# A graph-network kernel: all loops written out, seven gathers for every pair of groups, and the eighth tile divided between ScalarE, VectorE and SyncE

## What is computed

```python
msg_in = jnp.concatenate([nodes[row], nodes[col], edge_features], axis=-1)
messages = relu(msg_in @ mW1 + mb1) @ mW2 + mb2
aggregated = jax.ops.segment_sum(messages, col, num_segments=12500)
upd = relu(jnp.concatenate([nodes, aggregated], -1) @ uW1 + ub1) @ uW2 + ub2
out = layernorm(nodes + upd)          # over the 64 features, no affine part
```

## Time and profile before

| | |
|---|---|
| median of 3 runs | 1922.34 us (1921.92 to 1922.72) |
| profiled execution, own time | 1922.22 us |
| its span, first to last instruction | 1920.4 us |
| granted TensorE clock, mean share of full speed | 0.804 |
| busy in the span | VectorE 1540.8 us, POOL 1431.4, TensorE 1429.3, ScalarE 1242.0 |
| DMA | 229.86 MB, 120 GB/s, 44% of 16 engines' time from 100 us on |

### The profile page before, as it was taken

How to read it: one execution, slowest core, us unless ns; L and a number is a source line. 1 busy time by engine, 2 the same in 40 slices (tenths; PEclk the granted TensorE clock), 3 DMA queues, 4 the chain that set the end, 5 groups by cost and what they waited for, 6 DMA issues and landing times.

```text
span 1920.4 us, 56413 instructions
## 1 busy us (share of the span) xinstructions
PE 1429.3 (74%) x8716; PEld 1334.2 (69%) x8716; DVE 1540.8 (80%) x10793; ACT 1242.0 (65%) x10165; POOL 1431.4 (75%) x1527
## 2 busy tenths in 40 slices
PE   6776677777678777767768777776867878777877
PEld 6776566777667677666667667766767767766776
DVE  5568888888888888888888888888888888888883
ACT  3246766767766766766666666766666666766663
POOL 7777777777777777777777777777777777777773
PEclk8898888778877878788887887878788776877686
DMA  9664444444444444444444444444444444444441
GB/s 239 163 154 113 123 114 114 123 115 114 123 113 114 124 115 112 120 118 113 115 123 113 112 122 117 114 119 120 112 115 123 113 114 122 115 114 119 118 109 35
DMA packets 169379, 229.86 MB, mean 120 GB/s; under 512 B 98508, under 2 KB 117687, under 8 KB 168701
## 3 DMA queue, kind: packets, MB, share of 16 engines
q1 hardware_dynamic: 112484, 124.14, 23.4%
q0 software_dynamic: 48416, 97.68, 20.6%
q10 hardware_dynamic: 8254, 5.59, 1.2%
HBM read 217.59 MB, written 9.60 MB: 118 GB/s over the span
## 4 chain that ended last, share of the span: by engine, by line
POOL 63%; issue 23%; PE 4%; DVE 3%; DMA 3%; DVEq 1%; ACT 1%; POOLq 1%; SPq 1%; ACTq 0%
POOL gath L717 63%; DVE col_x L469 2%; DMA gath<-table_src,idx 1%; PE ps_sum L856 1%; DVEq L460 1%; DMA table_src<-gath 1%; PE ps_pre L824 1%; PE ps_pre L825 1%; DVE hid L1180 1%; PE ps_pre L790 0%; PE ps_pre L832 0%; POOLq L302 0%; DMA xwin<-in_xT_dram 0%; ACT hid L1000 0%; DMA col_src<-in_srcT_dram 0%
## 5 line engine op out<-in xcount | busy, mean ns | idle before, releaser
L717 POOL DMA_INDIRECT gath<-table_src,idx x1388 | 1309.6, 944 | 423.0 <-issue 420.6
L469 ACT COPY col_x<-xdeg 64x1 f32 x9428 | 912.4, 187 | 237.6 <-issue 219.6
L832 PE MATMUL ps_pre<-rhs,lhs 128*128 128x128 f32 x3226 | 603.0, 363 | 448.3 <-DVE lhs L1158 445.6
L469 DVE COPY col_x<-xdeg 64x1 f32 x9408 | 718.2, 138 | 216.0 <-issue 215.5
L832 PEld LDWEIGHTS ps_pre<-rhs,lhs 128*128 128x128 f32 x3226 | 558.8, 269 | 477.1 <-DVE lhs L1158 473.9
L856 PE MATMUL ps_sum<-onehot,hid 128*128 128x96 f32 x3322 | 473.2, 304 | 13.0 <-ACT rhs L976 11.9
L856 PEld LDWEIGHTS ps_sum<-onehot,hid 128*128 128x128 f32 x3322 | 463.3, 221 | 23.5 <-issue 15.2
L1007 ACT ACTIVATE hid<-hid 128x1024 f32<-128x1024 f32 x202 | 212.5, 1052 | 180.4 <-DVE hid L1180 177.0
L1180 DVE TENSOR_TENSOR hid<-ps_pre,gath 128x1024 f32<-128x1024 f32 x202 | 246.4, 1220 | 87.2 <-DMA gath<-table_src,idx 75.4
L1158 DVE TENSOR_SCALAR_CACHE_REDUCE lhs<-lhs,place 96x1024 f32<-96x1024 int32 x208 | 264.6, 1272 | 32.7 <-PE ps_sum L765 19.8
L1150 DVE TENSOR_TENSOR onehot<-ps_iota,dst_rel 128x768 f32<-128x768 f32 (+1 forms) x209 | 196.9, 943 | 0.1
(11 more groups left out here) (109 smaller groups left out, 639.1 us busy)
## 6 DMA issues: line engine op xcount, KB each, us to landing
lhs<-in_dst_dram SPq DMA_DIRECT2D x207, 384.0 KB
lhs<-in_edgeT_dram SPq DMA_DIRECT2D x207, 128.0 KB
gath<-table_src,idx POOLq DMA_INDIRECT x1388
table_src<-gath SPq DMA_DIRECT2D x12, 512.0 KB, 7.0
xwin<-in_xT_dram SPq DMA_DIRECT2D x208, 24.0 KB
idx<-in_srcT_dram SPq DMA_DIRECT2D x192, 4.0 KB
out_dram<-yout ACTq DMA_DIRECT2D x48, 64.0 KB, 1.6
col_src<-in_srcT_dram SPq DMA_DIRECT2D x148, 0.5 KB
```

Of the source, the lines that this page charges most:

```text
L469: ins = copy(col_x[:, i, start + n + j:start + n + j + 1], col)
L717: pool.indirect_dma_start(gath[0:m, k, j * H:(j + 1) * H], None, table_src, src_by_tile(p, k, j, m)).then_inc(gathered[k], 16)
L832: mm = nc.tensor.matmul(to[0:m, j * H:(j + 1) * H], lhs[:, k, j * P:j * P + m], rhs[:, k, :], start=True, stop=not by_cols)
```

## The change

Four things are done together.

1. The `Fori` loops go. SyncE, POOL and ScalarE are written out like the others, and every number in them is a constant.
2. From pair 13 on every pair has seven gathers, slot 0 too. Of the eighth tile ScalarE copies columns 0 to 63, VectorE 64 to 119 (24, then 32), and the last 8 rows come as 8 DMAs of one `table_src` row each, issued by SyncE straight into `gath` (`load_rows`). Their places in `col_x` are zero.
3. ScalarE makes all its 64 copies for pair p+2 in one step. It loads its registers sixteen at a time, the first sixteen at the end of the step before. VectorE makes 32 copies for pair p+1 in the first batch and 24 for pair p+2 in the second; the wait for the second batch stands ahead of `turned`.
4. The starts of the windows are loaded four registers at a time at every fourth pair, in `add_sums` and in `load_window`, and VectorE computes the two addresses for `add_sums` (`place_sums`) ahead of its first batch. Indices are loaded into eight slots (`AHEAD`) instead of four, seven pairs ahead.

```diff
-COL_K = (1, 2, 3)
-COL_PLAN = (((2, 0, 32), (1, 48, 16)), ((2, 32, 32), (0, 0, 16)), ((0, 16, 32), (0, 48, 16)), ((1, 0, 32), (1, 32, 16)))
+EARLY = 16
+COL_FROM = 13
 COL_TILE = PT - 1
+COL_ACT = 64
+COL_LOAD = 16
+COL_DVE = 24
+COL_ROWS = 8
+AHEAD = 2 * SLOTS
...
-        def copy_batch(eng, copy, i, start, count, done):
+        def load_regs(eng, k, start, count):
             regs = [eng.alloc_register(f"col{next(col_regs)}") for n in range(count)]
-            eng.load(regs, col_src[0:1, i, start:start + count])
+            for n in range(0, count, 32):
+                eng.load(regs[n:n + 32], col_src[0:1, k, start + n:start + min(n + 32, count)])
+            return regs
...
+        def wait_cols(eng, p):
+            k = p % SLOTS
+            eng.wait_ge(col_src_in[k], col_loads(p))
+            if col_before(p) is not None:
+                eng.wait_ge(pe_steps, steps_for_pre(col_before(p)))
+            let(eng)
...
@@ SyncE
-            def load_idx(p, it, k):
-                if not (isinstance(p, int) and p < (PEELED + 1) * SLOTS):
-                    sp.wait_ge(hsum_made, p - SLOTS + 1)
+            def load_idx(p):
+                if p >= EARLY + AHEAD:
+                    sp.wait_ge(hsum_made, p - AHEAD + 1)
...
+                    if k == 0:
+                        regs = [sp.alloc_register(f"start{p + i}") for i in range(SLOTS)]
+                        sp.load(regs, start_i[0:1, p:p + SLOTS])
...
+                p = it * SLOTS + k
+                if has_cols(p + SLOTS):
+                    load_cols(p + SLOTS, col_tile(p + SLOTS), P)
...
+                if EARLY <= p + AHEAD - 1 < PAIRS:
+                    load_idx(p + AHEAD - 1)
+                if has_rows(p + PREP):
+                    load_rows(p + PREP, (k + PREP) % SLOTS)
...
+            def load_rows(p, k):
+                sp.wait_ge(col_src_in[k], col_loads(p))
+                sp.wait_ge(hsum_made, p - SLOTS + 1)
...
+                regs = [sp.alloc_register(f"row{next(col_regs)}") for n in range(COL_ROWS)]
+                sp.load(regs, col_src[0:1, k, P - COL_ROWS:P])
+                for n, reg in enumerate(regs):
+                    src = sp.snap(reg, donate=True, min_val=0, max_val=N - 1)
+                    q = P - COL_ROWS + n
+                    sp.dma_start(gath[q:q + 1, k, COL_TILE * H:PW], table_src[bass.ds(src, 1), :]).then_inc(rows_in[k], 16)
...
@@ ScalarE, in step
-                copy_cols(act, nc.scalar.copy, it, k, 0, 0, cols_act)
-                copy_cols(act, nc.scalar.copy, it, k, 1, 0, cols_act)
+                if has_cols(p + 2):
+                    if p + 2 == COL_FROM:
+                        first_regs(p + 2, to)
+                    held = act_regs.pop() + load_regs(act, to, COL_LOAD, COL_LOAD)
+                    copy_batch(act, nc.scalar.copy, to, 0, held)
+                    for start in range(2 * COL_LOAD, COL_ACT, COL_LOAD):
+                        held = load_regs(act, to, start, min(COL_LOAD, COL_ACT - start))
+                        done = copy_batch(act, nc.scalar.copy, to, start, held)
+                    done.then_inc(cols_act, 1)
+                if p + 2 >= COL_FROM and has_cols(p + 3):
+                    first_regs(p + 3, (k + 3) % SLOTS)
...
@@ VectorE, in step
-                copy_cols(dve, nc.vector.tensor_copy, it, k, 0, COL_HALF, cols_dve)
+                if p % SLOTS == SLOTS - 1:
+                    load_starts(p - SLOTS + 1)
+                at = place_sums(p - 3) if p >= 3 else None
+                if has_cols(p + 1):
+                    to, start = (k + 1) % SLOTS, COL_ACT + COL_DVE
+                    held = load_regs(dve, to, start, P - COL_ROWS - start)
+                    done = copy_batch(dve, nc.vector.tensor_copy, to, start, held)
...
+                if has_cols(p + 2):
+                    wait_cols(dve, p + 2)
...
-                    add_sums(*pair(it, k, 3))
+                    add_sums(*pair(it, k, 3), at)
...
-                copy_cols(dve, nc.vector.tensor_copy, it, k, 1, COL_HALF, cols_dve)
+                if has_cols(p + 2):
+                    to = (k + 2) % SLOTS
+                    held = load_regs(dve, to, COL_ACT, COL_DVE)
+                    copy_batch(dve, nc.vector.tensor_copy, to, COL_ACT, held).then_inc(cols_dve, 1)
```

More of the change, by code:

```diff
@@ L236, in gnn_kernel @@
         idx_rest_in = sem("idx_rest_in")
-        idx_in = [sem(f"idx_in{i}") for i in range(SLOTS)]
+        idx_in = [sem(f"idx_in{i}") for i in range(AHEAD)]
         raw_got = [sem(f"raw_got{i}") for i in range(RAW)]
@@ L357, in steps_for_window, with pairs @@
             return p - 2
-        def pairs(eng, step, node, tail, peeled=PEELED, looped=True):
-            for it in range(peeled if looped else LAG):
+        def pairs(eng, step, node, tail):
+            for it in range(ITERS - 1):
                 for k in range(SLOTS):
                     step(it, k)
-            if looped:
-                with eng.Fori(peeled, LAG) as it:
-                    for k in range(SLOTS):
-                        step(it, k)
-            def both(it, c):
-                for k in range(SLOTS):
-                    step(it, k)
-                    for stage in STAGES[k]:
-                        node(c, stage, NP)
-            if looped:
-                with eng.Fori(LAG, ITERS - 1) as it:
-                    both(it, it - LAG)
-            else:
-                for it in range(LAG, ITERS - 1):
-                    both(it, it - LAG)
+                    if it >= LAG:
+                        for stage in STAGES[k]:
+                            node(it - LAG, stage, NP)
             def end(i, stage):
@@ L386, in end @@
                 node(c, stage, NP if c < CHUNKS else LAST, i)
-            both(ITERS - 1, ITERS - 1 - LAG)
+            for k in range(SLOTS):
+                step(ITERS - 1, k)
+                for stage in STAGES[k]:
+                    node(ITERS - 1 - LAG, stage, NP)
             end(0, UPD)
@@ L449, in copy_last, with has_cols @@
-        def copy_last(eng, copy, i, start, count, done):
-            eng.wait_ge(col_src_in[i], (ITERS - COL_FIRST + 1) * 16)
-            eng.wait_ge(pe_steps, steps_for_pre((ITERS - 1) * SLOTS + COL_K[i]) if i == 0 else steps_for_pre((ITERS - 2) * SLOTS + COL_K[i]))
-            let(eng)
-            copy_batch(eng, copy, i, start, count, done)
-        def copy_batch(eng, copy, i, start, count, done):
-            regs = [eng.alloc_register(f"col{next(col_regs)}") for n in range(count)]
-            eng.load(regs, col_src[0:1, i, start:start + count])
-            for n in range(0, count, COL_GROUP):
+        def has_cols(p):
+            return COL_FROM <= p < PAIRS
@@ new lines, in col_tile, with gathers_of, got, col_loads @@
+        def col_tile(p):
+            return LAST_ROWS if is_last(p) else COL_TILE
+        def gathers_of(p):
+            return rows_of(p) if is_last(p) else PT - has_cols(p)
+        def got(p):
+            return 16 * sum(gathers_of(q) for q in range(RAW, p + 1) if q % SLOTS == p % SLOTS)
+        def col_loads(p):
+            return 16 * sum(has_cols(q) for q in range(COL_FROM, p + 1) if q % SLOTS == p % SLOTS)
+        def col_batches(p):
+            return sum(has_cols(q) for q in range(COL_FROM, p + 1))
@@ L462, in copy_batch @@
+        def copy_batch(eng, copy, k, start, regs):
+            for n in range(0, len(regs), COL_GROUP):
                 of = []
@@ L829, in pre @@
                 for j, m in tiles_of(p):
-                    last = [i for i, tile, count in LAST_COLS if is_last(p) and tile == j]
-                    by_cols = last or j == COL_TILE and has_cols(it, k)
+                    by_cols = has_cols(p) and (j == col_tile(p) or j == TILES and is_last(p))
                     mm = nc.tensor.matmul(to[0:m, j * H:(j + 1) * H], lhs[:, k, j * P:j * P + m], rhs[:, k, :], start=True,
@@ L915, in _ @@
                 pe.wait_ge(rows_out[0], len(TABLE))
-                pairs(pe, step, node, tail, looped=False)
+                pairs(pe, step, node, tail)
             with pe.Else():
@@ L1011, in relu_last @@
                 act.wait_ge(pe_steps, steps_for_pre(p))
[L1012 removed]
+                for j, m in LAST_TILES:
                     at = slice(j * H, (j + 1) * H)
@@ L1252, in _ @@
             with dve.If(fit == 1):
-                pairs(dve, step, node, tail, looped=False)
+                pairs(dve, step, node, tail)
             with dve.Else():
```

198 lines of the change are left out of this document (91 added, 107 removed).

## The result

The changed kernel takes 1931.66 us (median of 6 runs, 1928.34 to 1940.63), the kernel before beside it 1922.13 (6 runs, 1921.10 to 1924.26). The profiled execution took 1940.63 us, the slowest of the six, its span 1938.7; the granted TensorE clock was 0.786 for 0.804 before.

A forecast was written before the change was run, and what follows sets the result against it. POOL's gathers bound the kernel before; VectorE would become the bound, its 8.66 us step plus 0.77 making 9.42. With 142.2 ahead, 192 steps and a 42.5 tail: 1993 us, 3.7% slower, range 1945 to 2050 (8 in 10).

The forecast's parts named there:

- rivals 2 and 3: SyncE (rival 2, chance 0.10) or ScalarE (rival 3, 0.08) becomes the bound: 9.6 to 9.8 us a step, 2028 to 2066 us.
- Rival 1: POOL stays the bound, faster: VectorE's step 8.2 to 8.5 us, below POOL's 8.75, time 1862 us; chance of faster 0.11.
- Rival 4: The two shifts cancel: VectorE at 9.05 us a step, 1918 to 1926 us; chance 0.03.
- Sum +0.77: a step of **9.42 us: VectorE's step: all terms together add 0.77 us, giving 9.42, 0.67 above POOL's new floor.
- 8 more copies, splits: VectorE's step: eight more copies at 0.074 us each, +0.60, and more splits from more instructions, +0.04.
- load of 24 registers for 16: VectorE's second batch: eight more registers at 62.6 ns each, exposed behind `turned`, +0.50 us.
- start's load and addresses leave: Between `turned` and VectorE's second batch: the start's load and address computations go, -0.75 us.
- addresses arrive ahead of the first batch: Ahead of VectorE's first batch, whose load isn't covered: address computations return, +0.20 us, bounds 0.12 and 0.26.
- four starts: VectorE's load of four starts in every fourth step: taken as 0.40 us, +0.10 a step, bounds 0.08 and 0.13.
- wait for columns, net: Wait now ahead of `turned` in every step, 0.14 us; before, three of eight batches had one: +0.05.
- `rows_in`: VectorE's step: one more condition to wait for, +0.03 us, from 0 to 0.05.
- So its own step is 9.05 - 0.39 = **8.66 us: VectorE's step before the change: POOL's pace of 9.05 us less 0.39 idle for gathers.

The follow-up runs named there:

- no_rows: The changed kernel without SyncE's row DMAs and without add_gathered's wait for them: 1929.78 us, ratio 1.0048.
- act_48: The changed kernel with ScalarE loading and copying 48 instead of 64 columns, the 16 left out zero: 1934.84 us, ratio 1.0053.
- rows12: The changed kernel with 12 instead of 8 rows by SyncE and 20 instead of 24 columns in VectorE's second batch: 2000.49 us, ratio 1.0381.
- v_8fewer: The changed kernel with VectorE loading and copying 16 instead of 24 columns in its second batch, 8 left zero: 1910.00 us, ratio 0.9921.
- starts_single_c: The changed kernel, window start loaded singly and addresses computed behind `turned`: 2058.82 us, ratio 1.0709; earlier as starts_single, when all kernels took some 3000 us, 0.9937 and 0.9908.
- place_late_c: The changed kernel with add_sums' addresses computed behind `turned` again, starts still loaded four at a time: 1939.04 us, ratio 1.0095.
- every16_c: The changed kernel with all eight tiles gathered in every sixteenth pair, whose `gath` tile is cleared after use: 1914.45 us, ratio 0.9935.

## Why the prediction was right in direction and wrong in size

**Right.** VectorE is the bound, POOL waits for it, and the steps from pair 12 to 204 make the time. The slack behind POOL was 0.39 us a step and the change uses more than that. Rows and ScalarE are hidden (no_rows, act_48), so rivals 2 and 3 are refuted for this kernel; both do exist one step on (rows12 at 9.48, v_8fewer at 8.96). Rival 1 fails by VectorE's 9.10 against POOL's floor of 8.75. Rival 4, both shifts cancelling at 9.05 and 1918 to 1926 us, came nearest: 0.05 a step off. I had given it 0.03.

**The step that failed** is the sum of the terms, "Sum +0.77: a step of **9.42 us**". VectorE's step came to 9.10, and from 8.65 (9.04 - 0.39) that is +0.45. Two terms of the sum and the step that it starts from were mis-sized:

| term | predicted | measured | read from |
|---|---|---|---|
| 8 more copies, splits | +0.64 | +0.63 | table of stretches |
| load of 24 registers for 16 | +0.50 | +0.51 | 1603 - 1097 ns |
| start's load and addresses leave | -0.75 | -0.84 | starts_single_c |
| addresses arrive ahead of the first batch | +0.20 | +0.12 | place_late_c |
| four starts | +0.10 | +0.08 | starts_single_c for place_late_c |
| wait for columns, net | +0.05 | +0.04 | see below |
| `rows_in` | +0.03 | +0.03 | no_rows |
| sum | +0.77 | +0.57 | |

*The start's load and the addresses*, net -0.55 in the prediction, are -0.72. The rows of before had the larger figure: the start's load begins at 169.9 and the load of columns behind it at 170.8, 0.9 us, where I added up durations to 0.75. And the addresses cost the same 0.12 in either place, by place_late_c; I had put the arrival at 0.20. That is 0.17 of the miss.

*The step that the sum starts from.* "So its own step is 9.05 - 0.39 = **8.66 us**" was read too high from a kernel that POOL holds back: the idle time that the profile puts to the gathers is not all that waiting for them costs. The kernel before shows it by itself, with the same instructions, once without a wait for gathers and once with one:

```profile
367.51 1.23 DVE L1180 TENSOR_TENSOR hid<-ps_pre,gath 128x1024 f32<-128x1024 f32 x1
...
369.77 0.87 DVE L469 COPY col_x<-xdeg 64x1 f32 x11 [0.17 <-issue]
...
439.21 1.22 DVE L1180 TENSOR_TENSOR hid<-ps_pre,gath 128x1024 f32<-128x1024 f32 x1 [0.94 <-DMA gath<-table_src,idx]
...
441.55 2.41 DVE L469 COPY col_x<-xdeg 64x1 f32 x32 [0.24 <-issue]
```

From hid to the first copy it is 2.26 us in the first and 2.33 in the second. In the first the load of 32 registers starts 0.01 us before `add_gathered`, in the second 0.06 after it. In the undisturbed steps from pair 16 to 26 the stretch is 2.26 or 2.41 us (without and with a wait for columns in it), and in the 160 steps of the table 2.33 or 2.48 by medians: 0.07 longer. So the bare step of before is some 8.58, and this is 0.07 of the miss.

*The wait for columns* was priced rightly, +0.05 for a measured +0.04, because the prediction had set the waits that go against the one that comes. Ahead of `turned` it costs 0.15 in every step (0.235 - 0.087); it left the first batch in the steps of k = 3 and 0 (2.48 for 2.33 us, 0.075 a step) and the second batch in that of k = 1 (2.46 for 2.31, 0.04 a step).

The terms as measured make 8.58 + 0.57 = 9.15, against 9.10. These 0.05 us, in the stretch from hid to the first copy, are not attributed. The bounds written beside the terms give only 9.29 to 9.53, not the 9.2 to 9.65 that I used, and the term -0.75 had no bounds at all.

**The rest of the sum.** The first steps came at 143.2 for 142.2. The tail was 48.0 us, not 42.5; in the other kernels it was from 35.5 (act_48) to 54.5 (v_8fewer), a spread that I had not foreseen. In the changed kernel TensorE waits 4.1 us in it for ScalarE's copy of a window, behind ScalarE's last batches. With 9.10 for the step, a mean that has the steps without `SCALE` in it, my own sum gives 142.2 + 1747.2 + 42.5 + 1.8 = 1933.7 us, the median within 0.1%. That is partly luck: the profiled execution is 9 us above the median, and no row says in which part the other executions were shorter.

The Trainium skill's rules on the sequencer (Runtime: NRT & Kernel Launch, "Instruction fetch mechanics") did no better behind the result than ahead of it. Its 200 ns for a register would make the load of 24 an estimated 4.8 us; the trace has 1.60. Its hidden fetch would leave no stop like the 0.31 us inside the second batch at 162.20. The changed kernel has 115 stops inside VectorE's batches (median 0.24 us). All but one of them come 128 of its instructions, or a multiple of that, behind the one before, to within one instruction. That they are fetch is my reading, which no run tests.

## What to carry to other kernels

When sequencer instructions leave a stretch, read their price from the start of the first to the start of what follows them, gaps included (0.9 us here), and not from their durations; and price the same instructions alike where they arrive. Read the own step of an engine that another holds back as an upper bound, since a register load behind a waiting instruction starts late too (0.07 us here). And when a change moves the bound from one engine to the next, don't take all of it: the gain of seven gathers was real but lay behind VectorE at 9.10, and one whole-gathered pair in eight puts POOL and VectorE both near 8.90, for 1.3% less than before.

## What the runs showed of the hardware that was not expected

- A DMA of one 512-byte row with a register in its address takes 228 ns to issue on SyncE (median of 1552), and 0.40 us with its register operations and gaps; the plain row took 451 ns.
- A register load that has no wait of its own can start before the data path begins the instruction ahead of it: in place_late_c at 155.528 us, with `add_gathered` starting at 155.573. With a wait for columns between them it starts 0.165 later than `add_gathered` (165.146 and 164.981 in the kernel before).
- An instruction that waits for the one just ahead of it holds back the register load behind it as well: the clearing of `gath` in every16_c, itself 0.17 us long, makes the next batch 1.3 us late.
- On two occasions all kernels took some 3000 us, over half as long again. In stretches single instructions then came 0.7 us apart on VectorE, whose copies are otherwise 0.07 apart, and such gaps are as frequent on ScalarE or more so, while gathers kept their 943 ns. The granted TensorE clock was 0.62 in starts_single. The cause stays open.
